# A gather engine that asks for a row only when the scan is fourteen rows behind it

## What is computed

```
h = xi[dst] + xj[src] + b_pre
mean = segment_sum(h, dst, N) / degc
mean_sq = segment_sum(h * h, dst, N) / degc
std = sqrt(relu(mean_sq - mean * mean) + EPS_VAR)
mx = segment_max(h, dst, N)
mn = segment_min(h, dst, N)
...
out = concatenate([x, agg, agg * amp, agg * att]) @ W_post + b_post
```

## Time and profile before

| what | us |
|---|---|
| median of 3 runs, unprofiled | 1782.25 |
| the three runs | 1787.49, 1782.25, 1782.1 |
| span of the profiled execution (its own time, first to last instruction) | 2193.7 |
| busy in it: PE / PEld / DVE / ACT / POOL | 1471.8 / 1048.3 / 1424.0 / 502.9 / 804.2 |
| all 688 gathers of the two scan stages, busy on POOL | 674.0 |
| POOL idle just before those gathers | 796.7 |

### The profile page before, as it was taken

The page is one execution under the profiler, slowest core; times in us unless marked ns, Lnnn a source line. Parts: engine busy times, 40 slices in busy tenths (PEclk is TensorE's granted clock), DMA queues, the critical chain, the costliest instruction groups (busy, mean ns, idle before and its releaser), DMA issues.

```text
span 2193.7 us, 30278 instructions
## 1 busy us (share of the span) xinstructions
PE 1471.8 (67%) x11250; PEld 1048.3 (48%) x11250; DVE 1424.0 (65%) x2879; ACT 502.9 (23%) x1074; POOL 804.2 (37%) x831
## 2 busy tenths in 40 slices
PE   0277777667854777678677755457777777877553
PEld 0166777657842444445444543324444445544432
DVE  7899999691066665557556645666655566665447
ACT  3367677300031011111111110310111111111101
POOL 4400000032015455455554523155454555546230
PEclk9889898878986898889898887868888888888777
DMA  5223333234433455455555531344554555555320
GB/s 116 89 120 138 146 138 138 83 112 148 135 106 98 156 177 169 145 176 194 181 172 168 177 112 54 98 150 160 176 171 151 192 173 178 196 165 158 109 89 24
DMA packets 126239, 309.36 MB, mean 141 GB/s; under 512 B 21744, under 2 KB 73408, under 8 KB 125742
## 3 DMA queue, kind: packets, MB, share of 16 engines
q1 hardware_dynamic: 75216, 145.00, 18.7%
q10 hardware_dynamic: 23470, 105.20, 13.7%
q0 software_dynamic: 27440, 57.77, 9.8%
HBM read 167.18 MB, written 140.75 MB: 140 GB/s over the span
## 4 chain that ended last, share of the span: by engine, by line
DVE 36%; PE 31%; another core or an unknown queue 16%; issue 8%; DMA 4%; ACT 2%; POOL 1%; ACTq 1%; DVEq 0%; SPq 0%; POOLq 0%
PE ps L1139 14%; PE ps L1267 6%; DVE accs L2141 5%; DVE scanned L2170 4%; DVE accs L2123 4%; DVE scanned L1682 3%; DVE scanned L1679 3%; DVE scanned L1688 3%; PE ps L1279 2%; DMA A<-counts 2%; PE ps L1164 2%; PE ps L1367 2%; PE ps L1432 1%; DVE S L1655 1%
## 5 line engine op out<-in xcount | busy, mean ns | idle before, releaser
L1078 POOL DMA_INDIRECT scanned<-table,rest_idx x688 | 674.0, 980 | 796.7 <-DMA rest_history<-scanned 327.9
L1139 PE MATMUL ps<-big,A 125*128 125x128 bf16 (+1 forms) x7500 | 772.5, 259 | 104.6 <-issue 81.8
L1139 PEld LDWEIGHTS ps<-big,A 125*128 125x128 bf16 x7500 | 623.6, 104 | 249.6 <-issue 139.8
L1267 PE MATMUL ps<-S,big 126*128 126x500 bf16 (+1 forms) x1050 | 282.1, 413 | 264.1 <-DVE accs L2141 184.2
L2141 DVE TENSOR_TENSOR accs<-accs,ps 128x1000 f32<-128x1000 f32 (+1 forms) x154 | 166.8, 1083 | 402.4 <-remote 313.5
L2170 DVE SCALAR_TENSOR_TENSOR scanned<-scanned,rest_neg 128x256 f32<-128x256 f32 x688 | 331.8, 482 | 32.5 <-issue 6.0
L1267 PEld LDWEIGHTS ps<-S,big 126*128 126x128 bf16 x1050 | 102.6, 107 | 387.8 <-DVE accs L2141 205.7
L1164 PE MATMUL ps<-scanned 128*128 128x150 bf16 x1050 | 116.2, 253 | 76.1 <-DVE scanned L1688 75.1
L2123 DVE TENSOR_TENSOR accs<-accs,ps 128x1000 f32<-128x1000 f32 (+1 forms) x154 | 166.0, 1078 | 1.8 <-DVE MS L1796 1.1
L1096 POOL IOTA Y<- 128x784 int32 x1 | 0.8, 786 | 362.8 <-DVEq L1944 362.8
L1164 PEld LDWEIGHTS ps<-scanned 128*128 128x128 bf16 x1050 | 87.6, 132 | 92.5 <-issue 73.2
(11 more groups left out here) (384 smaller groups left out, 1409.8 us busy)
## 6 DMA issues: line engine op xcount, KB each, us to landing
rest_history<-scanned SPq DMA_DIRECT2D x172, 512.0 KB
A<-counts ACTq DMA_DIRECT2D x75, 800.0 KB
S<-picks SPq DMA_DIRECT2D x60, 640.0 KB
picks<-S ACTq DMA_DIRECT2D x25, 800.0 KB
counts<-A ACTq DMA_DIRECT2D x25, 800.0 KB
scanned<-table,rest_idx POOLq DMA_INDIRECT x688
table<-Y SPq DMA_DIRECT2D x10, 320.0 KB, 2.6
S<-picks SPq DMA_DIRECT2D x10, 160.0 KB
```

The costliest lines, as they stand in the source:

```text
L1078: nc.gpsimd.indirect_dma_start(out=lanes[:, r, s, 0:F], out_offset=None, in_=tables[1 + l], in_offset=bass.IndirectOffsetOnAxis(ap=rest_id ...
L1139: m = nc.tensor.matmul(acc[:, bank, 0:width], A[0:NB, slot, a, :], XS[0:NB, a, c, 0:width], start=a == 0 and c == 0, stop=a == NT - 1 and ...
L1267: m = nc.tensor.matmul(ps[:, bank + h, 0:len(blocks) * NB], XS[0:NB + 1, a, c, 0:F], pick[0:NB + 1, part % RING, 0:len(blocks), a % PART, ...
```

## The change

POOL gets one more wait in front of each gather of row 14 and later: DVE must have scanned row i-14 of this layer. In the first layer `l * REST` is 0, in the second 344. The waits that were there stay.

```diff
+ROWS_LEAD = 14
...
                     for s in range(BATCH):
                         i = k * BATCH + s
+                        if i >= ROWS_LEAD:
+                            pool.wait_ge(main.scan_ops, l * REST + i + 1 - ROWS_LEAD)
                         nc.gpsimd.indirect_dma_start(
                             out=lanes[:, r, s, 0:F], out_offset=None, in_=tables[1 + l],
```

## The result

The changed kernel takes 1798.94 us in the median of four runs (1795.31 to 1801.92), the kernel before 1782.17 us beside it (1780.73 to 1787.49). The ratio is 1.0087 with a 95% interval of 1.0063 to 1.0111: slower by 16.8 us. That is inside the range given, which ended at 1799, by 0.06 us only, and it is not the likeliest case (no change, 1784, 0.46). In size it is nearest to the first rival, "POOL becomes the bound", at 1797 (0.30).

The account below looks back on a forecast made before the run. It took DVE and PE to set the middle of the scan stages, 357 us, hiding POOL's 350.5; all terms 0 except 1 us per stage, 2 us in all, taking 1782.25 to about 1784 us; range 1772 to 1799.

Parts of the forecast that it names:

- no change: Whole kernel: no difference that can be measured, 1784 us, or 1782 if the wait has no effect; chance 0.46.
- POOL becomes the bound: Rival, slots 8 to 77 of both stages: slower by at most 7.5 us per stage, 1797 us; chance 0.30.
- Added waits: New waits before 2 x 330 gathers on POOL: an already satisfied wait costs nothing, 0 us.
- How far ahead: Start of slot 8: 38 gathers issued instead of 44, 7.5 us of POOL's work moved to the middle; store waits become DVE waits.
- What a row needs: Issue to negation, 3.5 to 6.9 us, plus 0.63 us: hidden by ten rows of DVE's work, at least 8.8 us.
- What the middle needs: Slots 8 to 77: POOL's 343 us become 350.5, hidden under 357 us of DVE and PE; 1 us per stage allowed.
- ACT's queue: Copies and roots behind a later negation on ACT: covered by ACT's idleness, 0 us.
- The 411 us: Profiled execution's excess over the median run: mostly PE's slow stretches in the scan stages, which the timed run does not have.
- Gathers land too late: Rival, quick stretches of both middles: landings of 10 us stop DVE, about 20 us, 1802 us; chance 0.06.
- lower bound of 333.8 us for the middle: Slots 8 to 77 in a timed run: 436.5 us per stage less first slots and tail, all 411 us excess in the stages.
- Less crowding: Rival, loads of counts and picks: fewer gather bursts shorten PE's waits, some 8 us faster, 1774 us; chance 0.18.
- The wait never acts: Rival, whole timed run: POOL is never more than 14 ahead, so 1782 us; part of the 0.46 for no change.

Follow-up runs that it names:

- lead30: The change with ROWS_LEAD = 30 in place of 14, so the added waits are always satisfied already: 1782.86 us, ratio 1.0013 to the kernel before.
- early: The change with its new wait only on rows 14 to 59 of each layer: 1794.73 us, ratio 1.0085 to the kernel before.
- mid: The change with its new wait only from row 120 of each layer on: 1783.99 us, ratio 1.0015 to the kernel before.
- fewer: The kernel before without the fourth gather of each odd batch, 43 of 344 per layer: 2050.90 us, ratio 0.9389, where the kernel before takes 2176.91.
- front4: The kernel before, no cap, with four rows instead of three scanned in each of slots 0 to 7: 2133.25 us, ratio 0.9984, kernel before 2142.27.

## Why the prediction was right and wrong

The range holds, and that is luck: by 0.06 us, for a time that the prediction's own sum put at 1784. The step that failed is "At 357 us POOL's 350.5 us are hidden and the change costs 0". POOL needed 370.2 us, DVE and PE did not hide it, and the timed median rose by 16.8 us.

**Added waits: 0 us.** Nearly right: 1.9 us for all of them (`lead30`, 0.5 to 4.1 us by its interval).

**How far ahead.** Right to the gather: 44 becomes 38 at slot 8. Also right that the middle holds six gathers more, and that the store is never the last wait with the change. "The 327.9 us turn into waits for DVE" is wrong at this level, where there were 21.7 us to turn. These few were the ones that mattered: three of them, 7.0 us in layer 1, are POOL standing at the full ring right after slot 8, and the prediction counts the head start without them.

**What a row needs.** Half right. The landings are about as long as taken (6.52 and 7.85 us in the chain, where gather to negation was 3.5 and 6.9 us). But they are not covered by ten rows of DVE's work: they stand on the chain in both kernels. "Nobody waits for it to the end" rested on an execution in which PE was late. By the Trainium skill, DMA: Bandwidth & Descriptors, Rules for kernel authors, each DMA is to be issued early, and the runs agree in part: where the cap makes POOL ask later, on the first rows, 13.7 us are lost (`early`); where POOL is no further ahead than the cap allows, the cap costs nothing (`mid`).

**What the middle needs.** This is the step that failed, in the size of POOL's side.
- POOL's side was 272 x 1.25 + 3 = 343 us before; it is 366.5 us. The pitch came from twelve gathers; from row 60 on, with the DMA engines 0.75 busy in place of 0.53, it is 1.29 us, some 11 us more. When slot 78 starts, 324 gathers are out and not 316: landing, negation and ACT's slot of advance cover 8 gathers, some 10 us, and not 3. And some 6 us are waits for stores just after slot 8, which the sum hasn't got. After the change it is 370.2 us (and 372.8 us in layer 0), not 350.5.
- What DVE and PE need was taken as 357 us, from free slots of 5.10 us. Nothing in the profiles contradicts it, and no run tests it: `fewer`, which was to show it, fell on the other level. But it is under POOL's side and not over it. POOL was already the bound before the change.

The price, 7.5 us per stage, was near the timed one (8.4 us; 6.9 us in `early`), but for a reason that holds only in part. It supposes that all six gathers are lost at POOL's pitch. The windows to row 60 show 3.9 and 4.0 us, since before the change POOL lost part of its head start at the full ring. In the two profiles the middles grew by 6.7 and 3.7 us, 10.4 of the 12.2 us by which the spans differ. Why the timed difference is larger than what the windows show is open; the changed kernel's runs scatter from 1795.31 to 1801.92 us.

**ACT's queue: 0 us.** Wrong in kind. ACT waits 604.4 us for gathers in place of 515.1, and the root behind a negation stands in the chain. I read ACT's low busy share as cover, but ACT's program puts the root behind the negation, so its idle time there is the wait and covers nothing. Its share of the loss isn't priced separately; it is one of the ways on which a late batch reaches PE.

**The 411 us.** Half right and half wrong, and this misled the rest. Right: the runs timed beside the change have none of it. Wrong: "something that the timed run does not have". On other occasions all timed runs of the kernel before, 7 and 23 of them, are that slow. And most rows of the prediction (POOL's 1% of the chain, 59.3 us of ACT's waits, 0.53 of DMA) describe that level, not the one that was forecast. The lower bound of 333.8 us for the middle came from putting the whole excess into the two stages. Measured as the prediction did, from DVE's first `accs` to the last row, they take 467.1 and 465.0 us, in place of 2 x 436.5: 59 of the 411 us lie outside the stages.

**The rivals.** "POOL becomes the bound" had the place, the sign and the price, 15 us, and was given 0.30 where its own argument for it (POOL's cap used up in the quickest stretch, the estimate under 348 us) was stronger than the one against. By its own condition, a middle under 350.5 us, it would not have come true: the middle takes 366.5 us before. The condition used the same POOL side that was too small; what it had to ask is whether POOL needs more than DVE and PE do. "Gathers land too late" is not shown by any run: DVE's waits for a negated row grow only from 8.5 to 12.5 us, but no run delays landings where POOL keeps its lead. "Less crowding": PE's waits for the counts went from 16.4 us to 13.7 us, for the picks from 29.1 to 30.1 us. That is no gain of 8 us. "The wait never acts" is nearly true from row 120 on, where the cap costs nothing (`mid`).

## What to carry to other kernels

A producer that is "half idle" in a profile can still be the bound, if that execution was slowed elsewhere: first compare the profiled span with the timed median, and where they differ, rebuild the pace of each engine (count x pitch in the busiest stretch) against the shorter time. A ring buffer's depth is a reserve filled in the slow phase and spent in the fast one; count how many items are out at the border between the two. A cap costs at most those it takes away there, at the producer's pitch, less what the producer would have lost at the full ring (here 3.9 us seen of 7.9), and it is free where the producer is no further ahead than the cap. Where one program runs at two levels on different occasions, a change must be judged at both, because it can have opposite signs.

## What was not expected of the hardware

The same kernel takes 1781 us (1777.78 to 1787.57) on one occasion and 2177 or 2142 us on others, and all its runs on one occasion agree on the level. The chips differ, nothing in the kernel does: the first set of experiments ran on the chip numbered 6, the second on 9, the third on 4. Each was used once, so chip and occasion can't be told apart. The chip of the first comparison is not on record. At the slow level PE's matmuls of the sums come singly or stop, and DVE then waits up to 14 us for "remote". What holds PE up is open. The granted clock is lower too: over layer 1's middle it is 1.00 of full speed in before, 0.87 in `front4` and 0.90 in the change at the slow level. But it did not start the hold-up where that can be seen in detail. In the stretch of the earlier trace rows (PE alone; us, busy, clock, DMA share, GB/s) it is still 1.00, at 2.4 GHz, while the matmuls come singly, and falls to 0.50, 1.2 GHz, after:

```profile
948.30:953.00 4.70, 1.35 (x5) 1.00 0.21 56
953.00:955.40 2.40, 1.05 (x3) 0.64 0.10 27
955.40:960.00 4.60, 4.38 (x11) 0.50 0.48 113
```

And of the 502.9 - 366.5 = 136 us by which the middle of `front4` is longer than before's, PE is busy 379.0 - 344.6 = 34 us more; the rest is idleness. The idleness before the single matmuls is put down to "issue", that is to nothing the profile shows, so a late supply of PE's instructions is a possible cause that no run tests.

The hold-ups do depend on POOL and its gathers: an eighth of the gathers left out takes 6.1% off, 126 us for 86 gathers, more than their whole 1.3 us each; a cap on the lead takes 3.4% off with all gathers kept, and 2.1% more on top of the omission. Against a plain load on the DMA engines speaks that at the fast level they move more (250 GB/s in the middle, against 180 in `front4`) and PE is not held up; and in the stretch above the DMA engines are only 0.21 busy. Whether it is the burst of gathers after a store has landed, which a cap breaks into single ones, was not tried by itself.

Back-to-back indirect gathers of 128 rows of 512 bytes have a pitch of 1.25 us in short stretches and 1.29 us over 327 us with the DMA engines 0.75 busy; each is 0.94 to 1.0 us of POOL and a gap of 0.30 us.
